# Causal head attention: two of three key blocks centred on GpSimd, two PSUM banks swapped by sequence, four engines reordered

## The chip, the cores and the metric

The program runs on one core of a Trainium2 chip. The metric is the device time of one execution in microseconds (us). The engines are named as in the profile: PE is TensorE (matrix multiplications and transposes; PEld its weight loads), DVE is VectorE, ACT is ScalarE, POOL is GpSimd, SP is SyncE, which issues the DMAs. Each engine works through its own instructions in order, and waits on semaphores for the others.

## The reference, cut to what matters

The whole program is two transformer layers on 16 sequences of 256 tokens with 128 features. The change is inside the first attention only (`_L0_attn_ref`), which has 16 heads of 8 features and a causal mask; its output is added to `x`.

```python
def _L0_attn_ref(x, Wq, Wk, Wv, Wo):       # B=16, T=256, D_MODEL=128, N_HEADS=16, D_HEAD=8
    ...
            scores = scale * jnp.einsum('bhtd,bhsd->bhts', Q, kb)
            scores = jnp.where(future[None, None], -jnp.inf, scores)
            m_new = jnp.maximum(m, jnp.max(scores, axis=-1, keepdims=True))
            p = jnp.exp(scores - m_new)
            ...
            l = corr * l + jnp.sum(p, axis=-1, keepdims=True)
            acc = corr * acc + jnp.einsum('bhts,bhsd->bhtd', p, vb)
    ...
    return acc / jnp.maximum(l, 1e-12)     # then the projection with Wo
...
x = L0_attn_x
x = x + _L0_attn_ref(_layernorm(x, axis=-1), L0_attn_Wq, L0_attn_Wk, L0_attn_Wv, L0_attn_Wo)
```

## The kernel before

The function `head_attention` works through 16 sequences (b) of 4 rounds (j) each, so 64 rounds; a round does 4 of the 16 heads, which lie in 4 groups of 32 partitions. Queries are cut in two tiles of 128. Tile 0 sees key block 0 only, tile 1 sees blocks 0 and 1, so a round has three blocks of 128 keys for each of its 4 heads: 128 partitions x 4 x 384 values. In the tile `a_sc` they are numbered 0 (tile 0, diagonal), 1 (tile 1, key block 0, which needs no mask) and 2 (tile 1, diagonal).

The stages of one round r, with the lines of the profile:

- PE L371 computes the scores into PSUM banks 0 to 3 (16 products).
- DVE L456 adds the mask to blocks 0 and 2 and writes them to `a_sc`; ACT L511 copies block 1 there.
- DVE L444 takes the maxima of block 0 and L446 those of blocks 1 and 2. POOL L330 subtracts the maxima from block 0; DVE L448 subtracts them from blocks 1 and 2 (1024 values in each partition).
- ACT L507 takes the exponential of all three blocks.
- PE L357 transposes the result in three parts of 4 blocks; ACT L496 copies each part out of PSUM. Parts 0 and 2 share bank 4, part 1 has bank 5.
- PE L399 multiplies by the values and by ones (for the sums), and accumulates four rounds in bank 7, which L390 first clears.

Once in a sequence come the projections, all in bank 6: PE L339 and L340 (queries and keys), taken out by ACT L472 and L474 (five instructions); PE L347 (values), taken out by ACT L480; and at the end of a sequence ACT L487 and L489 (the inverse of the sums as logarithm and exponential), DVE L438 (`oT`, the product of accumulator and inverse), PE L414 (the output projection) and DVE L463 (the addition to `xT`). POOL L316 copies a sequence's input.

There is no scheduler. Each engine has its function `iteration`, whose written order is the order of its instructions, and `pipeline` calls it for every round. Rounds overlap by their lag: in the iteration of round r, PE does the scores of r, transposes r-2 and multiplies r-3 by the values; DVE does the maxima and the subtraction of r-1 and then the mask of r; ACT takes parts 0 and 1 of r-2, then the exponential of r-1, the copy of block 1 of r, and part 2 of r-2. In the text the iteration with j=3 is called the sequence's last, although the values of its fourth round are accumulated only in the iteration j=2 of the next one. There are two buffers each of `a_sc`, `a_pr` and `a_prT`, so the mask of r waits for the exponential of r-2 (`exped`).

Waits that matter here: the scores of r wait for the block 1 copy of r-1 (`copied`); the transposes of parts 0 and 1 wait for the exponential of their round and for part 2 of the round before (`taken`); the second maximum waits for the copy; the exponential waits for both subtractions (`centred0`, `centred1`); `oT` waits for the inverse.

Of the kernel before, what the change touches and what calls it, by code (L numbers as in the profile page):

```python
# [265 lines left out]
def head_attention(nc, sem, sb, xT, norm, banks, ident, w, head_mask, mask):  # L266
# [20 lines left out]
    def pipeline(eng, iteration):  # L287

        def one(j, k, b, live, more):
            iteration(j, k, b, lambda lag: b * ROUNDS + (j - lag + 1), live, more)  # L290
        for b in range(2):
            for j in range(ROUNDS):
                one(j, b, b, lambda lag: lag <= b * ROUNDS + j, True)
        with eng.Fori(1, B // 2 - 1) as i:
            for k in range(2):
                for j in range(ROUNDS):
                    one(j, k, i * 2 + k, lambda lag: True, True)
        for b in range(B - 2, B):
            for j in range(ROUNDS):
                one(j, b % 2, b, lambda lag: True, b < B - 1)  # L300
        for j in range(ROUNDS):
            one(j, 0, B, lambda lag: lag > j, False)
# [4 lines left out]
    with nc.Block() as block:  # L307
        @block.gpsimd
        def _(pool):
# [8 lines left out]
            nc.gpsimd.tensor_copy(xa[0][:], norm[:, 0:T]).then_inc(S["xcopy"], 1)  # L318

            def iteration(j, k, b, n, live, more):  # L320
                if more and j == 0:
                    if live(3):
                        copy(b + 1, 1 - k)
                    else:
                        nc.gpsimd.tensor_copy(xa[1 - k][:], norm[:, (b + 1) * T:(b + 2) * T])\
                            .then_inc(S["xcopy"], 1)
                if live(1):
# [4 lines left out]
                        .then_inc(S["centred0"], 1)  # L332
            pipeline(pool, iteration)

        @block.tensor
        def _(pe):
            def project(b, k):
                pe.wait_ge(S["xcopy"], passed(b + 1))
                nc.tensor.matmul(banks[:, 6, 0:T], w[:, 0, :], xa[k][:], start=True, stop=True)  # L339
                nc.tensor.matmul(banks[:, 6, T:2 * T], w[:, 1, :], xa[k][:], start=True, stop=True)\  # L340
                    .then_inc(S["proj"], 1)

            def project_values(b, k):
                pe.wait_ge(S["qmasked"], passed(b + 1))
                pe.sem_inc(sem("gate"), 1)
                for t in range(TILES):
                    last = nc.tensor.matmul(banks[:, 6, t * P:(t + 1) * P], xa[k][:, t * P:(t + 1) * P], w[:, 2, :],  # L347
# [3 lines left out]
            def iteration(j, k, b, n, live, more):  # L351
# [9 lines left out]

                if live(0):
# [20 lines left out]
                if live(3):  # L383
                    pe.wait_ge(S["taken"], passed(n(3) * 3))
                    if j3 == 0:
                        pe.wait_ge(S["vtaken"], passed((b if j == 3 else b - 1) + 1))
                        if live(7):
                            pe.wait_ge(S["odone"], passed(b if j == 3 else b - 1))
                        pe.sem_inc(sem("gate"), 1)
                        nc.tensor.matmul(banks[:, 7, :], zeros[:, 0:64].bitcast(BF16), zeros[:].bitcast(BF16),  # L390
                                         start=True, stop=False)
                    pe.sem_inc(sem("gate"), 1)
                    for t in range(TILES):
                        for add_up in range(2):
                            for s in range(4):
# [4 lines left out]
                                    banks[32 * s:32 * s + 32, 7, lo:lo + (2 - t) * P], stationary,  # L400
# [3 lines left out]
                if more and j == 1:  # L404
                    if live(5):
                        pe.wait_ge(S["added"], passed(b - 1))
                    project(b + 1, 1 - k)
                if more and j == 2:
                    project_values(b + 1, 1 - k)
                if live(4) and j == 3:  # L410
                    pe.wait_ge(S["odone"], passed(b))
                    pe.wait_ge(S["vtaken"], passed(b + 2 if more else B))
                    pe.sem_inc(sem("gate"), 1)
                    nc.tensor.matmul(banks[:, 6, 0:T], w[:, 3, :], oT[:], start=True, stop=True)\  # L414
# [12 lines left out]
        def _(dve):  # L427
# [4 lines left out]

            def iteration(j, k, b, n, live, more):
                if live(4) and j == 3:
                    dve.wait_ge(S["inverse"], passed(b))
                    if live(8):
                        dve.wait_ge(S["wo_done"], passed(b - 1))
                    nc.vector.tensor_tensor(oT[:], banks[:, 7, 0:T], rtotal[:], ALU.mult).then_inc(S["odone"], 1)  # L438
                if live(1):
                    c = (j - 1) % 2  # L440
                    dve.wait_ge(S["masked"], passed(n(1)))
                    if live(3):
                        dve.wait_ge(S["centred0"], passed(n(3)))
# [4 lines left out]
                    nc.vector.tensor_tensor(sc[c][:, :, P:3 * P], sc[c][:, :, P:3 * P],  # L448
                                            mx[c][:, 1].unsqueeze(2).broadcast_to([P, 4, 2 * P]), ALU.subtract)\
# [10 lines left out]
                if live(4) and j == 3:  # L460
                    dve.wait_ge(S["wo_done"], passed(b))
                    rows = xT[:, bass.ds(b - 1, 1), PAD:PAD + T].rearrange("p b t -> p (b t)")
                    nc.vector.tensor_tensor(rows, rows, banks[:, 6, 0:T], ALU.add).then_inc(S["added"], 1)  # L463
# [3 lines left out]
        def _(act):  # L467
            nc.scalar.preload_act_table_set("natural_log_exp_and_others")

            def take_queries_keys(b, k):  # L470
                act.wait_ge(S["proj"], passed(b + 1))
                nc.scalar.activation(kT[k][:], banks[:, 6, T:2 * T], ACT.Copy)  # L472
                for r in range(ROUNDS):
                    last = nc.scalar.activation(qm[k][:, r, :], banks[:, 6, 0:T], ACT.Copy,  # L474
# [3 lines left out]
            def take_values(b, k):  # L478
# [3 lines left out]
                    banks[:, 6, 0:TILES * P].rearrange("p (s j d) -> p s j d", j=ROUNDS, d=AD), ACT.Copy)\  # L482
                    .then_inc(S["vtaken"], 1)

            def invert(b):
                act.wait_ge(S["valued"], passed(b * ROUNDS))
                nc.scalar.activation(rtotal[:], banks[:, 7, T:2 * T], ACT.Ln).then_inc(S["logged"], 1)  # L487
# [3 lines left out]
            def iteration(j, k, b, n, live, more):  # L491
# [6 lines left out]

                if live(2):
# [4 lines left out]
                if live(1):  # L504
                    act.wait_ge(S["centred0"], passed(n(1)))
                    act.wait_ge(S["centred1"], passed(n(1)))
# [1059 lines left out]
```

## Time and profile before

| what | value |
|---|---|
| time, median of 3 runs | 4096.82 us (4094.83 to 4099.13) |
| the profiled execution, its own time | 4096.23 us |
| its span | 4094.3 us |
| head attention, from its first product to the last addition | 48.75 to 425.30 us, 376.55 us |
| busy in that stretch: PE, DVE, ACT, POOL | 307.19, 283.00, 266.95, 71.52 us |
| granted clock of TensorE in that stretch | 0.93 of full speed |
| granted clock in the rest (425.30 to 4094.30 us) | 0.99 |

The changed stage is 9% of the span. No engine is busy throughout in it. The profiled time is what the device took; the span runs from the first to the last recorded instruction, and 1.9 us lie around it. In the timeline rows, `x8` means that eight instructions of one kind in a row are merged, the second number is the length of that merged piece, and the number in brackets is the idle time of that engine before it, with the instruction that ended it. Start times of neighbouring rows on one engine give the true rate, since the next instruction is started a little before the record of the last one ends.

### The profile page before, as it was taken

Reading aid. Unit: us, or ns where it says so; the run is one execution under the profiler, and the core shown is the slowest. Engines: PE = TensorE matmul, PEld = TensorE weight load, DVE = VectorE, ACT = ScalarE, POOL = GpSimd, SP = SyncE. Lnnn points to the kernel's source line nnn. Section 1 sums busy time; section 2 is a strip of 40 time slices with the busy share of each in tenths; the row PEclk is TensorE's granted clock in tenths of the full one; section 3 lists DMA queues with packets and bytes.
Section 4 is the critical chain, followed back from the end, with each engine's and each line's share of the span. In section 5 each row is a group of like instructions: output and inputs, shape, how many; then the busy total and the mean of one; then the engine's idle time right before and its main releaser. Section 6 shows DMA issues by size and latency. Waiting matters only on the chain. (4 is left out here: it accounts for less than half of the span.)

```text
span 4094.3 us, 155009 instructions
## 1 busy us (share of the span) xinstructions
PE 3825.7 (93%) x61323; PEld 2408.6 (59%) x61339; DVE 3160.2 (77%) x4956; ACT 2971.3 (73%) x6599; POOL 2421.4 (59%) x2354
## 2 busy tenths in 40 slices
PE   5888688899999999999999999999999999999998
PEld 3555477466654666645666546666456665466663
DVE  4777455799975899947999658999489996699984
ACT  4777221788876888867888768888678887688885
POOL 2121133588862788826888538888178885378870
PEclk8999899899999999999999999999999999999999
DMA  2000000000000000000000000000000000000000
GB/s 74 0 0 1 0 0 0 7 0 0 0 22 6 1 0 0 0 21 7 0 0 0 21 6 0 0 0 0 22 7 0 0 0 21 7 0 0 0 19 24
DMA packets 12345, 27.32 MB, mean 7 GB/s; under 512 B 2461, under 2 KB 6729, under 8 KB 11345
## 3 DMA queue, kind: packets, MB, share of 16 engines
q1 hardware_dynamic: 12240, 25.72, 1.8%
q8 instruction: 91, 1.49, 0.2%
q14 instruction: 14, 0.11, 0.0%
HBM read 23.62 MB, written 2.10 MB: 6 GB/s over the span
## 5 line engine op out<-in xcount | busy, mean ns | idle before, releaser
L945 POOL TENSOR_TENSOR w_t<-w_t 128x512 f32<-128x512 f32 x768 | 978.4, 1283 | 514.3 <-DVE w_t L1247 514.3
L1247 DVE TENSOR_TENSOR w_t<-banks,w_tab 128x512 f32<-128x512 f32 x1536 | 955.9, 684 | 234.4 <-ACT w_sq L1385 225.7
L961 POOL TENSOR_TENSOR w_t<-w_t,w_rn 128x512 f32<-128x512 f32 x768 | 784.3, 1042 | 252.3 <-ACT w_rn L1422 252.3
L1039 PE MATMUL banks<-w_qk,w_xs 128*128 128x512 f32 x1536 | 825.6, 620 | 7.6 <-issue 6.5
L1059 PE MATMUL banks<-w_vo,w_xs 128*32 128x256 f32 x12288 | 822.8, 385 | 4.9 <-ACT w_us L1376 4.9
L1047 PEld LDWEIGHTS banks<-ident,w_t 128*128 128x128 f32 x3072 | 380.1, 140 | 432.7 <-issue 413.6
L1376 ACT ACTIVATE w_us<-banks 128x512 f32<-128x512 f32 x768 | 456.7, 595 | 161.7 <-PE banks L1059 157.0
L1047 PE MATMUL banks<-ident,w_t 128*128 128x128 f32 x3072 | 461.7, 273 | 25.6 <-POOL w_t L961 16.7
L1284 DVE TENSOR_REDUCE w_ss<-w_sq 128x16 f32<-128x1024 f32 x384 | 464.9, 1211 | 0.0
L1059 PEld LDWEIGHTS banks<-w_vo,w_xs 128*32 128x32 f32 x12288 | 321.6, 109 | 242.7 <-issue 77.0
L966 POOL TENSOR_TENSOR w_pr<-w_pr,w_rl 128x512 f32<-128x512 f32 x384 | 402.3, 1048 | 85.6 <-ACT w_rl L1427 85.6
L1098 PE MATMUL banks<-w_us,w_prT 128*32 128x128 f32 x10752 | 407.7, 273 | 6.1 <-issue 6.1
L1117 PEld LDWEIGHTS banks<-w_kT,w_qT 64*32 64x32 f32 x24576 | 319.1, 105 | 160.2 <-issue 160.2
L1098 PEld LDWEIGHTS banks<-w_us,w_prT 128*32 128x32 f32 x10752 | 349.1, 110 | 81.0 <-issue 18.9
L1117 PE MATMUL banks<-w_kT,w_qT 64*32 64x64 f32 x24576 | 381.2, 219 | 0.0
L1385 ACT ACTIVATE w_sq<-banks 128x512 f32<-128x512 f32 x384 | 229.2, 597 | 198.9 <-PE banks L1039 189.3
L1265 DVE TENSOR_TENSOR w_pr<-banks,w_mx 128x256 f32<-128x256 f32 x768 | 290.4, 420 | 22.1
L1288 DVE TENSOR_REDUCE w_tot<-w_pr 128x8 f32<-128x512 f32 x384 | 263.4, 686 | 56.6 <-ACT w_pr L1414 37.3
L1019 PE MATMUL banks<-logv,m_w 128*114 128x512 f32 x576 | 280.0, 622 | 23.1 <-DVE logv L1224 23.1
L1393 ACT ACTIVATE w_sq<-banks 128x512 f32<-128x512 f32 x384 | 229.7, 598 | 82.7 <-PE banks L1039 82.7
L1039 PEld LDWEIGHTS banks<-w_qk,w_xs 128*128 128x128 f32 x1536 | 231.1, 190 | 94.1 <-issue 94.1
L1259 DVE TENSOR_REDUCE w_mx<-banks 128x8 f32<-128x512 f32 x384 | 265.6, 692 | 13.0
(178 smaller groups left out, 5940.1 us busy)
## 6 DMA issues: line engine op xcount, KB each, us to landing
w_qk<-w_qk_in SPq DMA_DIRECT2D x7, 1024.0 KB, 4.8
w_v<-w_v_in SPq DMA_DIRECT2D x7, 512.0 KB, 5.6
w_o<-w_o_in SPq DMA_DIRECT2D x7, 512.0 KB, 6.3
m_w<-m_w_in SPq DMA_DIRECT2D x6, 342.0 KB
xT<-x_in SPq DMA_DIRECT2D x4, 512.0 KB
out<-kept SPq DMA_DIRECT2D x8, 256.0 KB, 2.4
m_w<-m_w_in SPq DMA_DIRECT2D x6, 171.0 KB
r_tab<-r_tab_in SPq DMA_DIRECT2D x1, 512.0 KB
```

What stands on the lines that cost most here:

```text
L945: nc.gpsimd.tensor_tensor(v1, v1, v2[:, :, ::-1, :], ALU.add).then_inc(S["added"], 1)
L961: nc.gpsimd.tensor_tensor(v1, v1, rn[j % 2][:, i * HALF:(i + 1) * HALF].unsqueeze(2) .broadcast_to([P, HALF, WD]), ALU.mult).then_inc(S["n ...
L966: nc.gpsimd.tensor_tensor(p[:], p[:], rl[j % 2][:].unsqueeze(1).unsqueeze(3) .broadcast_to([P, 2, HALF, WIN]), ALU.mult).then_inc(S["weigh ...
L1039: nc.tensor.matmul(banks[:, i, :], x[:], wqk[:, i * INNER + hh * C:i * INNER + (hh + 1) * C], start=True, stop=True).then_inc(S["qk"], 1)
L1047: last = nc.tensor.transpose(banks[:, 3 + i, g * P:(g + 1) * P], t1[j1 % 2][:, lo:lo + P], ident[:])
L1059: last = nc.tensor.matmul(banks[WIN * g:WIN * (g + 1), 2, lo:lo + 2 * P], x[:, WIN * w:WIN * (w + 1)], wvo[:, first:first + 2, :].rearrang ...
L1098: last = nc.tensor.matmul(banks[WIN * w:WIN * (w + 1), 7, 0:P], prT[:, chunk, WIN * w:WIN * (w + 1)], rhs, start=(hv == 0 and i == 0), sto ...
L1117: last = nc.tensor.matmul(bank[WIN * w:WIN * (w + 1), g], qT[j1 % 2][rows, g, WIN * w:WIN * (w + 1)], kT[rows, hk * NPAIR + g, lo:lo + 2 * ...
L1247: nc.vector.tensor_tensor(dst[j % 2][:, i * C:(i + 1) * C].rearrange("p (h d) -> p h d", d=WD), src, tab[:, 2 * t + cs, i * WD:(i + 1) * W ...
L1265: nc.vector.tensor_tensor(pr[j2 % 2][:, :, par * NPAIR:(par + 1) * NPAIR].rearrange("p a g r -> p g a r"), heads[:, par], mx[j2 % 2][:, pa ...
L1284: nc.vector.tensor_reduce(ss[j % 2][:], sq[:].rearrange("p a h d -> p (a h) d"), AX, ALU.add)\
L1376: nc.scalar.activation(us[j][:, 2 * a:2 * a + 2].rearrange("p w a n -> p (w a n)"), banks[:, 2, :], ACT.Copy).then_inc(S["u_taken"], 1)
```

## The change

It touches only `head_attention`.

- **Subtraction.** POOL subtracts from block 0 and from block 1 (two instructions of 512 values in each partition, new L327 and L331), DVE only from block 2 (512 values, new L451). `centred0` counts two for each round.
- **Banks.** The accumulator of a sequence with buffer k lies in bank 6+k, and the projections for it lie in bank 7-k. The output projection goes to the bank that the sequence's own accumulator had.
- **POOL.** The inputs of two sequences are copied ahead, not of one.
- **ACT.** The block 1 copy of r comes before the exponential of r-1, not after it. The inverse moves from the end of iteration j=2 to the head of iteration j=3, where it stands before the copies of the transposed parts (the same place in the stream).
- **PE.** The query and key projections of the next sequence move from the tail of iteration j=1 to the head of j=2, before the scores. The part 2 transposes come before the value projection and the output projection, not after them.
- **DVE.** `oT` moves from the head of iteration j=3 to its tail, after the mask. The addition to `xT` moves to the head of iteration j=2 of the sequence after the next.

The core of the diff:

```diff
@@ gpsimd
+            for b in range(2):
+                nc.gpsimd.tensor_copy(xa[b][:], norm[:, b * T:(b + 1) * T]).then_inc(S["xcopy"], 1)
...
+                if more == 2 and j == 0:
+                    copy(b + 2, k)
                 if live(1):
...
+                    pool.wait_ge(S["maxed"], passed(n(1) * 2))
+                    nc.gpsimd.tensor_tensor(sc[c][:, :, P:2 * P], sc[c][:, :, P:2 * P],
+                                            mx[c][:, 1].unsqueeze(2).broadcast_to([P, 4, P]), ALU.subtract)\
+                        .then_inc(S["centred0"], 1)
@@ tensor
+                if more and j == 2:
+                    if live(6):
+                        pe.wait_ge(S["added"], passed(b - 1))
+                    project(b + 1, 1 - k)
                 if live(0):
...
-                        nc.tensor.matmul(banks[:, 7, :], zeros[:, 0:64].bitcast(BF16), zeros[:].bitcast(BF16),
+                        nc.tensor.matmul(banks[:, 6 + k3, :], zeros[:, 0:64].bitcast(BF16), zeros[:].bitcast(BF16),
...
-                if more and j == 1:
-                    if live(5):
-                        pe.wait_ge(S["added"], passed(b - 1))
-                    project(b + 1, 1 - k)
+                if live(2):
+                    pe.wait_ge(S["taken"], passed(n(2) * 3 - 2))
+                    pe.sem_inc(sem("gate"), 1)
+                    turn(2)
                 if more and j == 2:
                     project_values(b + 1, 1 - k)
                 if live(4) and j == 3:
                     pe.wait_ge(S["odone"], passed(b))
-                    pe.wait_ge(S["vtaken"], passed(b + 2 if more else B))
...
-                if live(2):
-                    pe.wait_ge(S["taken"], passed(n(2) * 3 - 2))
-                    pe.sem_inc(sem("gate"), 1)
-                    turn(2)
@@ vector
+            def add(b, k):
+                dve.wait_ge(S["wo_done"], passed(b + 1))
+                rows = xT[:, bass.ds(b, 1), PAD:PAD + T].rearrange("p b t -> p (b t)")
+                nc.vector.tensor_tensor(rows, rows, banks[:, 6 + k, 0:T], ALU.add).then_inc(S["added"], 1)
...
+                if j == 2 and live(10):
+                    add(b - 2, k)
...
-                    nc.vector.tensor_tensor(sc[c][:, :, P:3 * P], sc[c][:, :, P:3 * P],
-                                            mx[c][:, 1].unsqueeze(2).broadcast_to([P, 4, 2 * P]), ALU.subtract)\
+                    nc.vector.tensor_tensor(sc[c][:, :, 2 * P:3 * P], sc[c][:, :, 2 * P:3 * P],
+                                            mx[c][:, 1].unsqueeze(2).broadcast_to([P, 4, P]), ALU.subtract)\
...
+                if j == 3 and not live(0):
+                    add(b - 1, 1 - k)
```

ACT, inside the loop, from the part 2 copy of iteration j=2 to that of iteration j=3 (`a_v`: values, `a_rtotal`: logarithm and inverse, `a_prT`: transposed parts, `a_pr`: exponential, `a_sc`: block 1). Before:

```order
L496 ACTIVATE a_prT<-banks 128x512 [waits a_turned]
L480 ACTIVATE a_v<-banks 128x32x8 [waits a_vproj]
L487 ACTIVATE a_rtotal<-banks 128x256 [waits a_valued,a_odone]
L489 ACTIVATE a_rtotal<-a_rtotal 128x256 [waits a_logged]
L496 ACTIVATE a_prT<-banks 128x512 [waits a_turned] x2
L507 ACTIVATE a_pr<-a_sc 128x1536 [waits a_centred1,a_centred0]
L511 ACTIVATE a_sc<-banks 128x4x128 [waits a_masked]
```

Changed:

```order
L502 ACTIVATE a_prT<-banks 128x512 [waits a_turned]
L486 ACTIVATE a_v<-banks 128x32x8 [waits a_vproj]
L493 ACTIVATE a_rtotal<-banks 128x256 [waits a_valued,a_odone]
L495 ACTIVATE a_rtotal<-a_rtotal 128x256 [waits a_logged]
L502 ACTIVATE a_prT<-banks 128x512 [waits a_turned] x2
L516 ACTIVATE a_sc<-banks 128x4x128 [waits a_masked]
L521 ACTIVATE a_pr<-a_sc 128x1536 [waits a_centred1,a_centred0]
```

Only the last two have changed places; the inverse stands where it stood.

DVE, inside the loop, iteration j=3 of a sequence (`a_mx`: maxima, `a_oT`: the product with the inverse). Before:

```order
L438 TENSOR_TENSOR a_oT<-banks,a_rtotal 128x256 [waits a_wo_done,a_inverse]
L444 TENSOR_REDUCE a_mx<-a_sc 128x4 [waits a_centred0,a_masked]
L446 TENSOR_REDUCE a_mx<-a_sc 128x4 [waits a_copied]
L448 TENSOR_TENSOR a_sc<-a_sc,a_mx 128x4x256 [waits a_maxed]
L456 TENSOR_TENSOR a_sc<-banks,a_mask 128x4x2x128 [waits a_exped,a_scored]
L463 ISA [waits a_wo_done]
L463 TENSOR_TENSOR xT<-xT,banks 128x256
```

Changed:

```order
L447 TENSOR_REDUCE a_mx<-a_sc 128x4 [waits a_centred0,a_masked]
L449 TENSOR_REDUCE a_mx<-a_sc 128x4 [waits a_copied]
L451 TENSOR_TENSOR a_sc<-a_sc,a_mx 128x4x128 [waits a_maxed]
L459 TENSOR_TENSOR a_sc<-banks,a_mask 128x4x2x128 [waits a_exped,a_scored]
L467 TENSOR_TENSOR a_oT<-banks,a_rtotal 128x256 [waits a_wo_done,a_inverse]
```

`oT`, which stood ahead of the maxima, stands behind the mask, the subtraction is half as wide, and the addition has left this iteration.

## Rows read from the trace of the kernel before

**Rows 1.** The profile's page, its first line.

```profile
span 4094.3 us, 155009 instructions
```

**Rows 2.** Windows: length; busy (instructions) of PE, PEld, DVE, ACT, POOL; PE's clock; DMA.

```profile
48.75:425.30 376.55, 307.19 (x4000) 214.96 (x4016) 283.00 (x288) 266.95 (x448) 71.52 (x79) 0.93 0.00 1
84.97:401.71 316.74, 261.97 (x3495) 183.81 (x3498) 246.72 (x252) 231.32 (x388) 62.65 (x69) 0.95 0.00 1
203.20:226.11 22.91, 19.38 (x252) 13.39 (x252) 17.68 (x19) 16.75 (x28) 4.50 (x5) 0.93 0.00 0
226.11:248.13 22.02, 17.82 (x252) 12.64 (x252) 17.69 (x19) 16.53 (x28) 4.50 (x5) 1.00 0.00 0
```

**Rows 3.** Timeline of ACT, 224 to 244 us: start, length, engine, line, instruction, [idle before].

```profile
224.23 0.66 ACT L496 ACTIVATE a_prT<-banks 128x512 f32<-128x512 f32 x1
...
226.11 1.09 ACT L496 ACTIVATE a_prT<-banks 128x512 f32<-128x512 f32 x2 [0.22 <-PE banks L357]
...
233.24 1.09 ACT L496 ACTIVATE a_prT<-banks 128x512 f32<-128x512 f32 x2 [1.22 <-PE banks L357]
234.21 1.49 ACT L507 ACTIVATE a_pr<-a_sc 128x1536 f32<-128x1536 f32 x1
235.59 0.60 ACT L511 ACTIVATE a_sc<-banks 128x512 f32<-128x512 f32 x1
236.06 0.61 ACT L496 ACTIVATE a_prT<-banks 128x512 f32<-128x512 f32 x1
237.89 1.09 ACT L496 ACTIVATE a_prT<-banks 128x512 f32<-128x512 f32 x2 [1.22 <-PE banks L357]
...
241.26 0.60 ACT L496 ACTIVATE a_prT<-banks 128x512 f32<-128x512 f32 x1 [0.43 <-PE banks L357]
...
243.45 1.12 ACT L496 ACTIVATE a_prT<-banks 128x512 f32<-128x512 f32 x2
```

**Rows 4.** The same timeline, DVE and POOL, 225 to 240 us.

```profile
225.92 0.42 DVE L438 TENSOR_TENSOR a_oT<-banks,a_rtotal 128x256 f32<-128x256 f32 x1 [3.46 <-ACT a_rtotal L489]
...
228.00 0.40 POOL L316 COPY a_x<-norm 128x256 f32 x1
228.10 1.38 DVE L448 TENSOR_TENSOR a_sc<-a_sc,a_mx 128x1024 f32<-128x1024 f32 x1
...
235.98 1.04 POOL L330 TENSOR_TENSOR a_sc<-a_sc,a_mx 128x512 f32<-128x512 f32 x1 [3.33 <-DVE a_mx L444]
...
236.22 1.22 DVE L446 TENSOR_REDUCE a_mx<-a_sc 128x4 f32<-128x1024 f32 x1 [0.31 <-ACT a_sc L511]
...
237.47 1.23 DVE L448 TENSOR_TENSOR a_sc<-a_sc,a_mx 128x1024 f32<-128x1024 f32 x1
...
238.61 1.22 DVE L456 TENSOR_TENSOR a_sc<-banks,a_mask 128x1024 f32<-128x1024 f32 x1
...
239.86 0.69 DVE L444 TENSOR_REDUCE a_mx<-a_sc 128x4 f32<-128x512 f32 x1
```

**Rows 5.** The same timeline, PE, 228 to 243 us.

```profile
228.38 0.70 PE L414 MATMUL banks<-a_oT,a_w 128*128 128x256 f32 x2
...
232.55 1.09 PE L357 MATMUL banks<-ident,a_pr 128*128 128x128 f32 x8
...
235.01 0.66 PE L357 MATMUL banks<-ident,a_pr 128*128 128x128 f32 x4
...
239.66 0.70 PE L339 MATMUL banks<-a_x,a_w 128*128 128x256 f32 x2
...
240.63 0.60 PE L357 MATMUL banks<-ident,a_pr 128*128 128x128 f32 x4
241.16 0.94 PE L371 MATMUL banks<-a_kT,a_qm 32*128 32x128 f32 x16
242.03 1.09 PE L357 MATMUL banks<-ident,a_pr 128*128 128x128 f32 x8
```

**Rows 6.** The page's groups of instructions: forms, count | busy us, mean ns | idle before.

```profile
L1247 DVE TENSOR_TENSOR w_t<-banks,w_tab 128x512 f32<-128x512 f32 x1536 | 955.9, 684 | 234.4 <-ACT w_sq L1385 225.7
```

More of the change, by code:

```diff
@@ L292, in pipeline @@
             for j in range(ROUNDS):
-                one(j, b, b, lambda lag: lag <= b * ROUNDS + j, True)
+                one(j, b, b, lambda lag: lag <= b * ROUNDS + j, 2)
         with eng.Fori(1, B // 2 - 1) as i:
@@ L337, in project @@
             def project(b, k):
+                bank = 7 - k
                 pe.wait_ge(S["xcopy"], passed(b + 1))
-                nc.tensor.matmul(banks[:, 6, 0:T], w[:, 0, :], xa[k][:], start=True, stop=True)
-                nc.tensor.matmul(banks[:, 6, T:2 * T], w[:, 1, :], xa[k][:], start=True, stop=True)\
+                nc.tensor.matmul(banks[:, bank, 0:T], w[:, 0, :], xa[k][:], start=True, stop=True)
+                nc.tensor.matmul(banks[:, bank, T:2 * T], w[:, 1, :], xa[k][:], start=True, stop=True)\
                     .then_inc(S["proj"], 1)
@@ L460, in iteration @@
                 if live(4) and j == 3:
-                    dve.wait_ge(S["wo_done"], passed(b))
-                    rows = xT[:, bass.ds(b - 1, 1), PAD:PAD + T].rearrange("p b t -> p (b t)")
-                    nc.vector.tensor_tensor(rows, rows, banks[:, 6, 0:T], ALU.add).then_inc(S["added"], 1)
+                    dve.wait_ge(S["inverse"], passed(b))
+                    if live(8):
+                        dve.wait_ge(S["wo_done"], passed(b - 1))
+                    nc.vector.tensor_tensor(oT[:], banks[:, 7 - k, 0:T], rtotal[:], ALU.mult).then_inc(S["odone"], 1)
+                if j == 3 and not live(0):
+                    add(b - 1, 1 - k)
             pipeline(dve, iteration)
@@ L471, in take_queries_keys @@
                 act.wait_ge(S["proj"], passed(b + 1))
-                nc.scalar.activation(kT[k][:], banks[:, 6, T:2 * T], ACT.Copy)
+                nc.scalar.activation(kT[k][:], banks[:, 7 - k, T:2 * T], ACT.Copy)
                 for r in range(ROUNDS):
-                    last = nc.scalar.activation(qm[k][:, r, :], banks[:, 6, 0:T], ACT.Copy,
+                    last = nc.scalar.activation(qm[k][:, r, :], banks[:, 7 - k, 0:T], ACT.Copy,
                                                 scale=head_mask[:, r:r + 1])
@@ L497, in take @@
                                          banks[:, 4 + part % 2, :], ACT.Copy).then_inc(S["taken"], 1)
+                if live(4) and j == 3:
+                    if live(8):
+                        act.wait_ge(S["odone"], passed(b - 1))
+                    invert(b, 1 - k)
                 if live(2):
@@ L512, in iteration @@
                         .then_inc(S["copied"], 1)
+                if live(1):
+                    act.wait_ge(S["centred0"], passed(n(1) * 2))
+                    act.wait_ge(S["centred1"], passed(n(1)))
+                    nc.scalar.activation(columns(pr[j1 % 2]), columns(sc[j1 % 2]), ACT.Exp, scale=A_SCALE)\
+                        .then_inc(S["exped"], 1)
                 if live(2):
```

47 lines of the change are left out of this document (13 added, 34 removed).

## The prediction, made before the changed kernel ran

> **What bounds the kernel now.** I read the page's first line for the whole [rows 1], then windows to find the stage, then its timeline for one sequence. The stage that is changed takes 376.55 of 4094.3 us, and everything behind it starts when it ends, so a microsecond saved here is one saved in all. In the stage no engine is full: PE is busy 307 of 376.55 us, DVE 283, ACT 267 [rows 2]. So waits set the pace, and the question is which. The second window runs from one copy of part 0 (iteration j=2 of the second sequence) to the same copy 14 sequences later: 316.74/14 = 22.62 us for a sequence. The third and fourth show single sequences: 22.91 us where PE's granted clock was 0.93, 22.02 us where it was 1.00 [rows 2]. A sequence without a clock dip is therefore 22.02 us, with 17.82 us of PE work, 17.69 of DVE and 16.53 of ACT.
>
> Cut at the ACT copies of parts 0 and 1, this sequence has rounds of 7.13 us (226.11 to 233.24), 4.65 (to 237.89), 5.56 (to 243.45) and the rest, 4.68 (to 248.13, the end of the fourth window) [rows 2, 3].
>
> The plain round, 4.65 us, is a ring of DVE and ACT: second maximum 1.25 (236.22 to 237.47), subtraction 1.14 (to 238.61), exponential, block 1 copy, second maximum. ACT stands idle 1.22 us in it [rows 3, 4]. The exponential starts 0.97 us after the part copies although its data are ready about then, and the block 1 copy, on which both the next maximum and the next scores wait, is queued behind it.
>
> The long round, 7.13 us, comes from the inverse. `oT` stands at the head of DVE's iteration, and DVE is idle for 3.46 us before it [rows 4], because ACT reaches logarithm and inverse only behind the exponential, the copy, part 2 and the values. After that stall the whole softmax of the round is late, and PE with it.
>
> **The change, part by part.** *The ring on ACT and PE.* With the copy ahead of the exponential, the DVE part leaves the ring, and the ring that is left is this one: part 2 copy, PE transposes parts 0 and 1, ACT copies them, block 1 copy, exponential, part 2 copy. Its pieces: the part 2 copy lasts 0.60 (241.26 to 241.86), PE starts 0.17 later (242.03), ACT can start 0.69 after PE (232.55 to 233.24) [rows 3, 5]; the two copies 0.97 (233.24 to 234.21), the block 1 copy 0.47 (235.59 to 236.06), the exponential 1.38 (234.21 to 235.59) [rows 3]. The sum is 4.28 us for a plain round against 4.65.
>
> *The other three rounds by the same ring.* In iteration j=1 the query and key copies fill the gap between part 2 and part 0: 2.19 us from one to the other (241.26 to 243.45) in place of 1.46, so 4.28 + 0.73 = 5.01 [rows 3]. The projections now stand behind part 2's transposes on PE, which makes them ready about 0.15 later than ACT wants them (an estimate from PE's pieces below): I take 5.16. In j=2 the values and the inverse fill the gap: 1.88 us (224.23 to 226.11), of which 0.22 is a wait for PE [rows 3] that the earlier scores take away, so 1.66: 4.28 + 0.20 = 4.48. In j=3 ACT alone would give 4.28. PE is late there: its plain round is 2.46 (232.55 to 235.01) + 0.53 (240.63 to 241.16) + 0.87 (241.16 to 242.03) = 3.86; the output projection with 0.70 and its overlap [rows 5], taken at 0.53, and the clearing of the bank, at about 0.3 from the same kind of gaps, make 4.7 against a start that is up to 0.15 early from the round before. I take 4.55. Sum: 4.28 + 5.16 + 4.48 + 4.55 = 18.47, say **18.5 us for a sequence**. PE's 17.82 us is the floor under it [rows 2].
>
> *`oT` and the addition.* At the tail of j=3 the inverse is long there, since ACT makes it before part 0 of that iteration and DVE reaches `oT` after a maximum, another, a subtraction and a mask. The stall of 3.46 us is gone and not replaced: what is queued behind the new wait is the next maximum (0.63 us of work that has 0.5 us to spare). What is late next is the output projection, which now waits for `oT` behind the mask, and the scores of the next round behind it on PE. By the positions above the mask ends 0.3 us after part 0's copy starts, `oT` 0.42 us later, PE wants it at 2.5: covered by well over 1 us. If that cover were gone, each 0.1 us would cost 0.1 us once in a sequence. The deferred addition (0.42 us) releases the projections at the head of j=2; it ends about 0.9 us after part 0's copy, PE arrives at 2.3. Cost nothing, cover 1.2 us.
>
> *DVE's load.* A round is now 0.63 + 1.25 + x + 1.25, the last from mask to maximum (238.61 to 239.86) [rows 4], with x the subtraction of 512 values. The trace has none with this form. Half of 1.14 is 0.57; the 128x512 form from PSUM took 0.684 [rows 6]. I take 0.65, the nearer in shape, and the ends are 0.57 and 1.14 (no gain at all). DVE needs 3.8 us (3.7 to 4.3) of 4.28, so even the upper end is only just a bound. The mask is done 0.57 us before ACT comes to its copy.
>
> *GpSimd.* It gets 1.04 us more in each round [rows 4], 2.1 of 4.28 and the input copy of 0.40. The second subtraction starts with the end of the second maximum, at 2.9 after part 0's copy, and ends at 4.0; the exponential of that round starts at 4.28 + 1.44 = 5.7. The cover is 1.7 us, so its price is nothing, unless it holds up DVE (below). Both subtractions are released by the same maximum: DVE starts 0.03 us after it (237.44 to 237.47), POOL some 0.07 after its own (235.91 to 235.98) [rows 4], so DVE is first. POOL held up by DVE's 0.65 us would still be in time.
>
> In the trace one DVE subtraction met a POOL instruction: the input copy ran from 228.00 to 228.40, and the subtraction that started at 228.10 took 1.38 us in place of 1.23 [rows 4], 0.15 more for 0.30 of overlap. The Trainium skill (SBUF — State Buffer, section "SBUF: two separate sides") says that a VectorE operation with two SBUF inputs and a GpSimd operation that reads SBUF exclude each other for the whole instruction, and that the one that starts first has it. By this rule the row should show the full 0.30; it shows half of it. Under the rule DVE's new subtraction is such an operation and GpSimd's second one starts beside it, so the sum would be the same where DVE is first, and the first rival below where GpSimd is.
>
> *PE's clock.* The third window shows a sequence with a dip (0.93), the fourth one without; the dips cost 22.62 - 22.02 = 0.60 us a sequence in the mean [rows 2]. PE's idle time in a sequence falls from 22.02 - 17.82 = 4.2 us to 0.7, and what starved it longest (the 3.46 us stall of DVE) is gone. I take these 0.60 us as gained. Kept, they would cost 14 x 0.6 = 8 us.
>
> *The sum.* 14 sequences x (22.62 - 18.5) = 57.7 us. Outside that window are 59.8 us [rows 1, 2], the fill and the drain, with about seven rounds in which 0.3 to 0.4 us each is saved, and one more inverse whose stall goes (taken at 2): 5 us, with 2 to 7 as its ends. The start has also a reverse: the first exponential now waits for GpSimd's second subtraction, about 1 us. Together 62 us. The profiled execution took 4096.2 us; 4096.2 - 62 = 4034.2, and its time is 0.6 below the median, so about **4035 us**. Its own range: from 18.1 us for a sequence (ACT's ring without PE's two delays), 4029, to 19.0 us, 4042.
>
> **The rivals.**
>
> *GpSimd first.* If GpSimd's second subtraction holds DVE's up, a ring over DVE appears: block 1 copy 0.60, second maximum 1.25, 0.07 + 1.04 for GpSimd, subtraction 0.65, mask 1.25: 4.86 us a round. A sequence is then 3 x 4.86 + 5.16 + 0.4 for `oT` = 20.1, the gain 14 x 2.5 + 3 = 38, the time 4059. For it: the 0.15 us above. Against it: DVE's earlier start, and that an overlap cost half of itself. Chance 15%. The rule of the Trainium skill named above is this rival's mechanism.
>
> *Waits that add up.* With PE at 17.82 of 18.5 us there is little room, and each handover that is 0.05 to 0.1 us longer than in my rows shifts the ring. At 19.5 us a sequence: 14 x 3.1 + 4 = 47, the time 4049. Branches of the loop (six times in 14 sequences), now hidden in PE's idle stretch, would be in the open as well. Chance 17%.
>
> *The clock stays low: slower.* PE becomes the bound; work at the lower of its two levels, 1.2 GHz in place of 2.4, takes twice as long. 17.82 x (1 + f) = 22.62 gives f = 0.27: if over 27% of the stage's PE work ran at the lower level, the kernel would be slower than before; at 50% a sequence is 26.7 and the time 4096 + 14 x 4.1 = 4153. Against it: a sequence in which PE was busy for only 17.82 of 22.02 us ran at 1.00 [rows 2], and the ones to come leave PE less idle time. Chance 4%.
>
> *The change doesn't remove the stall but moves it.* If the output projection waited for `oT` as long as `oT` waited for the inverse, a sequence would be about 22 us and the time within 8 us of before. My positions leave over 1 us of cover. Chance 4%.
>
> **How the numbers follow.** Forecast 4035 with 60%, GpSimd first (4059) 15%, added waits (4049) 17%, clock 4%, moved stall 4%. The range takes the forecast's lower end, 4028, and reaches over the first two rivals to 4060; what is left out is the slower cases and the extremes of the others, under 2 in 10. A measurement of this kernel can tell about 0.2%, 8 us, from no change. Faster by more than that: all but the last two rivals and a margin, 0.92; within it 0.03; slower 0.05.
>
> **What the profile of the changed kernel would show.** A stage of about 315 us; a sequence of 18.5 us between copies of part 0; no idle time of DVE before `oT`; plain rounds of 4.3 us with ACT idle 0.86 us before part 0 and PE idle 0.4; the second maximum, not the subtraction, as DVE's waiting place; PE's clock above 0.97 after the first sequence; the two GpSimd subtractions at 1.04 us, the second perhaps 0.6 longer. It is wrong if DVE's narrow subtraction shows more than 1 us (the first rival), if PE's clock falls below 0.9, or if the output projection is what ends PE's longest waits.

## The result and the profile after

The changed kernel takes 4026.10 us (median of 4 runs, 4023.78 to 4030.75), the kernel before 4095.82 us (median of 4, 4091.16 to 4099.13). The ratio is 0.983, with a 95% interval of 0.982 to 0.985. That is 69.7 us less, where 62 were forecast, and 1.9 us below the lower end of the stated range (4028).

The profiled execution took 4030.75 us, the slowest of the four. The windows of its trace, cut as in [rows 2]; columns are the window, its length, then busy time and instructions of PE, PEld, DVE, ACT and POOL, and PE's clock:

```profile
48.62:355.00 306.38, 286.75 (x4000) 199.85 (x4016) 250.33 (x288) 260.49 (x448) 170.46 (x143) 0.98 0.00 1
82.06:335.20 253.14, 244.78 (x3497) 171.57 (x3510) 218.89 (x253) 225.46 (x389) 148.70 (x124) 1.00 0.00 1
203.86:221.97 18.11, 17.55 (x252) 12.30 (x252) 15.64 (x19) 16.21 (x28) 10.67 (x10) 1.00 0.00 0
355.00:4028.80 3673.80, 3506.00 (x57291) 2188.42 (x57291) 2865.16 (x4645) 2692.10 (x6132) 2339.26 (x2260) 0.98 0.02 5
```

The stage fell from 376.55 to 306.38 us, by 70.2, which is the whole difference of the medians. The 14 sequences of the second window take 253.14/14 = 18.08 us each in place of 22.62, which gives 63.5 us; fill and drain, outside it, went from 59.8 to 53.2 us and give the other 6.6. PE is busy 97% of that window at a clock of 1.00, where it was 0.95. The rest of the program took 3673.8 us in this execution and 3669.0 in the profiled one of before; the other three executions have spans 4.6 to 7.0 us shorter, so nothing is explained by that.

One sequence on ACT (start, length, instruction, idle time before it), the counterpart of [rows 3]:

```profile
202.44 0.61 ACT L502 ACTIVATE a_prT<-banks 128x512 f32<-128x512 f32 x1
203.86 1.09 ACT L502 ACTIVATE a_prT<-banks 128x512 f32<-128x512 f32 x2 [0.81 <-PE banks L359]
204.83 0.60 ACT L516 ACTIVATE a_sc<-banks 128x512 f32<-128x512 f32 x1
205.31 1.50 ACT L521 ACTIVATE a_pr<-a_sc 128x1536 f32<-128x1536 f32 x1
206.68 0.61 ACT L502 ACTIVATE a_prT<-banks 128x512 f32<-128x512 f32 x1
...
208.89 1.11 ACT L502 ACTIVATE a_prT<-banks 128x512 f32<-128x512 f32 x2
...
211.70 0.66 ACT L502 ACTIVATE a_prT<-banks 128x512 f32<-128x512 f32 x1
...
213.26 1.07 ACT L502 ACTIVATE a_prT<-banks 128x512 f32<-128x512 f32 x2
...
217.73 1.09 ACT L502 ACTIVATE a_prT<-banks 128x512 f32<-128x512 f32 x2 [1.06 <-PE banks L359]
```

The rounds are 5.03 us (203.86 to 208.89), 4.37 (to 213.26), 4.47 (to 217.73) and 4.24 (to 221.97, the end of the third window). They had been 5.56, 4.68, 7.13 and 4.65. The block 1 copy follows the part copies at once, and ACT's only idle time is in front of part 0.

DVE and POOL in the same stretch, the counterpart of [rows 4]:

```profile
202.48 0.69 DVE L451 TENSOR_TENSOR a_sc<-a_sc,a_mx 128x512 f32<-128x512 f32 x1
202.52 1.55 POOL L331 TENSOR_TENSOR a_sc<-a_sc,a_mx 128x512 f32<-128x512 f32 x1 [0.28 <-DVE a_mx L449]
...
212.44 1.23 DVE L459 TENSOR_TENSOR a_sc<-banks,a_mask 128x1024 f32<-128x1024 f32 x1
...
213.58 0.41 DVE L467 TENSOR_TENSOR a_oT<-banks,a_rtotal 128x256 f32<-128x256 f32 x1
```

`oT` starts without any idle time before it; its 3.46 us are gone. GpSimd's second subtraction takes 1.55 us where the first takes 1.04: it starts 0.04 us after DVE's and is stretched by it, while DVE's takes 0.69.

### The profile page after: what moved, and what is told of

It reads as the page before. It is cut to its first block and busy times, and to the rows that moved or that the text cites. A ratio compares the mean times of both kernels' runs of the same rounds, so it can differ in the third digit from the quotient of the medians.

```text
span 4028.8 us, 155156 instructions
## 1 busy us (share of the span) xinstructions
PE 3808.7 (95%) x61323; PEld 2394.8 (59%) x61339; DVE 3127.4 (78%) x4956; ACT 2966.2 (74%) x6599; POOL 2520.9 (63%) x2418
```

## Experiments

Each was run beside the kernel before on the same chip. The changed kernel's 18.1 us for a sequence and 4026.1 us in all are what single undone parts are to be held against. "For a sequence" is the mean distance, in the trace, between the part 0 copies of iteration j=2 over 14 sequences, the first of them the short first sequence; for the changed kernel this mean is 18.10, for the kernel before 22.48. The rest of the program, which no run changes, took 3663 to 3674 us in the fourteen profiled executions, and the median of the kernel before was 4095.0 to 4099.2 us beside the different experiments. So a difference of a few us between two medians tells little, and the length of the stage in the trace (first product to last addition, 306.4 us in the changed kernel) tells more.

**DVE subtracts two blocks again.**

```diff
-  gpsimd: second subtraction, block 1
-  vector: sc[c][:, :, 2 * P:3 * P] -= mx[c][:, 1]
+  vector: sc[c][:, :, P:3 * P] -= mx[c][:, 1]
```

> The changed kernel with one part undone: DVE subtracts blocks 1 and 2 again (1024 values in each partition), GpSimd block 0 only. My theory: the changed kernel runs on a ring of ACT and PE at 18.1 us for a sequence, and DVE has about 0.5 us a round to spare (its own work is 3.8 us a round of 4.2); the wider subtraction takes 0.5 us more, which about fills that. 18.1 to 18.6 us for a sequence, the whole 0 to 8 us slower than the changed kernel (about 4030). Rival, the gain came from the work taken off DVE: then 19.5 us and more for a sequence, over 20 us slower.

4026.94 us, 18.26 us for a sequence. The part that gives the change its name is worth 0.16 us a sequence, 2 us in all, too little for the medians to show; the stage is 309.1 us, 2.8 longer. The rival (DVE's load) is out.

**The exponential first on ACT.**

```diff
-  scalar: copy of block 1 (round r); exponential (round r-1)
+  scalar: exponential (round r-1); copy of block 1 (round r)
```

> The changed kernel with one part undone: ACT takes the exponential before the block 1 copy, as before the change. My theory: the second maximum, GpSimd's subtraction, the exponential and the copy are a ring again, 1.25 + 0.07 + 1.55 + 1.38 + 0.63 = 4.9 us a round in place of 4.24 to 4.47, so about 19.9 us for a sequence and 25 to 30 us more in all (about 4054). Rival, the order on ACT does not matter since the copy is small: within 5 us of the changed kernel.

4051.17 us, 19.78 us for a sequence: 25 us more, as the theory had it. The rounds that begin in j=3 and j=0 are 4.88 and 4.95 us in its trace (208.81 to 213.69 and to 218.64), where 4.9 was expected.

**Fixed banks.**

```diff
-  accumulator in banks[:, 6 + k], projections in banks[:, 7 - k]
+  accumulator in banks[:, 7], projections in banks[:, 6]
-  pe.wait_ge(S["added"], passed(b - 1))      # before clearing the accumulator
+  pe.wait_ge(S["odone"], passed(b if j == 3 else b - 1))
```

> The changed kernel with one part undone: the accumulator is always in bank 7 and all projections in bank 6, so that clearing the accumulator for a new sequence waits for oT of the last one, which now stands behind the mask on DVE. My theory: PE clears the bank at about 214.1 us in the changed kernel's timeline in place of 213.4, and has no slack to make it up: 0.7 to 0.8 us more for a sequence, 18.8 to 18.9, 11 to 13 us in all (about 4038). Rival, the bank swap is idle, since PE would wait there anyway: within 3 us of the changed kernel.

4040.87 us, 18.85 us for a sequence, 0.75 more. The stage is 318.1 us, 11.7 longer, as expected; the median is 14.8 us higher, outside the 11 to 13 expected, with single times from 4035.0 to 4045.2. PE waits for `oT` before it clears the bank (total, times, longest, from 82.92 to 328.88 us):

```profile
PE banks L396 <- DVE a_oT L467: 8.3, 13, 0.7
```

That is 0.64 us a sequence, most of the 0.75. The swap matters, and mostly by the time for which clearing the bank is late.

**`oT` first on DVE.**

```diff
-  vector, j == 3: maxima, subtraction, mask, oT
+  vector, j == 3: oT, maxima, subtraction, mask
```

> The changed kernel with one part undone: oT stands at the head of DVE's iteration j=3 again, ahead of the maxima. My theory: DVE stops for the inverse, which ACT makes just before the part 0 copy of that iteration; the mask of that round is done 3.5 to 3.9 us later than ACT wants it, and that is the larger part of the whole gain: 21.6 to 22 us for a sequence, 52 to 60 us more in all (about 4082). Rival, most of the gain is the shorter ring of every round: then at most 25 us more.

4087.9 us, 22.19 us for a sequence: 61.8 us more, nearly all of the gain back. Its longest waits (who waited, for whom; total, times, longest), from 90 to 380 us:

```profile
DVE a_oT L446 <- ACT a_rtotal L495: 53.1, 13, 4.1
...
ACT a_sc L516 <- DVE a_sc L464: 40.3, 13, 3.1
...
PE banks L377 <- ACT a_sc L516: 23.1, 12, 1.9
```

The stall passes from DVE to the block 1 copy on ACT and on to PE's scores: 4.1, 3.1, 1.9 us. The sequence is a little longer than expected, and PE's clock fell again in some sequences. The windows of two of them, one without a fall and one with:

```profile
173.76:194.83 21.07, 17.82 (x253) 12.35 (x251) 15.40 (x19) 16.32 (x29) 10.70 (x9) 1.00 0.00 0
217.15:240.53 23.38, 20.47 (x253) 13.85 (x251) 15.50 (x19) 16.54 (x29) 10.69 (x9) 0.85 0.00 0
```

At 1.00 the sequence is 21.07 us, and with the dip it is 23.38.

**GpSimd subtracts all three blocks.**

```diff
-  gpsimd: sc[c][:, :, P:2 * P] -= mx[c][:, 1];  vector: sc[c][:, :, 2 * P:3 * P] -= mx[c][:, 1]
+  gpsimd: sc[c][:, :, P:3 * P] -= mx[c][:, 1]
```

> The changed kernel with GpSimd subtracting blocks 1 and 2 as well as block 0 and DVE none. It removes the overlap of a DVE subtraction with a GpSimd one. My theory: the exponential has 2.9 us from the end of the second maximum, GpSimd needs 0.07 + about 2.1 us, and DVE's time is not on the ring: 18.0 to 18.1 us for a sequence, within 3 us of the changed kernel. Rival, GpSimd holds up DVE or the exponential in the changed kernel: then this differs by more than 5 us, faster where DVE was held up, slower where GpSimd's time is on the path.

4024.44 us, 18.10 us for a sequence, the same as the changed kernel. The groups of this run (mean ns after the bar), then of the changed kernel, from 60 to 340 us:

```profile
L331 POOL TENSOR_TENSOR a_sc<-a_sc,a_mx 128x1024 f32<-128x1024 f32 x63 | 119.2, 1893 | 30.6 <-DVE a_mx L449 30.3
```

```profile
L331 POOL TENSOR_TENSOR a_sc<-a_sc,a_mx 128x512 f32<-128x512 f32 x63 | 97.3, 1545 | 29.7 <-DVE a_mx L449 29.5
L327 POOL TENSOR_TENSOR a_sc<-a_sc,a_mx 128x512 f32<-128x512 f32 x62 | 64.5, 1040 | 85.0 <-DVE a_mx L447 85.0
...
L451 DVE TENSOR_TENSOR a_sc<-a_sc,a_mx 128x512 f32<-128x512 f32 x62 | 42.9, 692 | 2.1
```

Without a DVE subtraction beside it, GpSimd does twice the width in 1.89 us; beside one it needs 1.55 for the single width. Neither shows in the time.

**One more ACT instruction, on the ring and in the gap.** Both add a copy of constants (512 in each partition) to a spare tile in two of four rounds.

```diff
                     take(0)
                     take(1)
+                    if live(4) and j in (3, 0): copy of constants     # the run "on the ring"
...
                     take(2)
+                if live(4) and j in (3, 0): copy of constants         # the run "in the gap"
```

> The changed kernel with one more ACT instruction (a copy of 512 constants in each partition to a spare tile, about 0.5 us from start to start) in iterations j=3 and j=0, between the part copies and the block 1 copy, which by my theory is on the ring. Theory: each adds its 0.5 us, 1.0 us for a sequence, 14 to 16 us in all (about 4041). Rival, PE alone is the bound, and ACT has slack everywhere: under 5 us in all. Its twin puts the same instruction where ACT is idle.

> The changed kernel with the same extra ACT instruction as its twin on the ring (512 constants, about 0.5 us, in iterations j=3 and j=0), but after the part 2 copy, where ACT stands idle for 0.8 to 1.06 us while PE transposes. Theory: hidden, 18.1 us for a sequence. Rival, ACT's total work is the bound: 19.1 us for a sequence.

On the ring: 4035.85 us, 18.90 us for a sequence. In the gap: 4023.48 us (2 runs), 18.13 us for a sequence. The instruction moves the block 1 copy by 0.52 us each time:

```profile
206.31 1.08 ACT L503 ACTIVATE a_prT<-banks 128x512 f32<-128x512 f32 x2 [0.81 <-PE banks L360]
207.28 0.63 ACT L516 ACTIVATE a_spare<-a_w 128x512 f32<-128x512 f32 x1
207.80 0.60 ACT L519 ACTIVATE a_sc<-banks 128x512 f32<-128x512 f32 x1
```

So the place decides, not ACT's total work. But two of them cost 0.80 us, not 1.04. The round that begins in iteration j=0 grew from 4.24 to 4.76 us, by the full 0.52; the one that begins in j=3 only from 4.47 to 4.74. In that one PE is late anyway behind the output projection, and 0.25 us were hidden. The cost is 9.8 us by the medians, 12.9 by the length of the stage (319.3 us), where 14 to 16 were expected.

**Banks 4 and 5 exchanged from round to round.** Then part 0 goes to the bank that part 1 had in the round before, which is free earlier.

```diff
-  banks[:, 4 + part % 2, ...]
+  banks[:, 4 + (part + j2) % 2, ...]           # transposes and part copies
-                        pe.wait_ge(S["taken"], passed(n(3) * 3))
+                        pe.wait_ge(S["taken"], passed(n(3) * 3 - 1))
                     turn(0)
+                    if live(3): pe.wait_ge(S["taken"], passed(n(3) * 3))
                     turn(1)
```

> The changed kernel with banks 4 and 5 exchanged from round to round, so that the transposes of part 0 need not wait for the part 2 copy of the round before. Theory: this opens the ring (part 2 copy, 0.6, and its handover no longer stand before PE's transposes), and PE's own work of 17.8 us is the bound: 17.8 to 17.9 us for a sequence in place of 18.08, 3 to 5 us faster in all (about 4022). Rival, the ring is not closed through the part 2 copy: no change in the sequence's time.

4014.67 us (4013.28 to 4015.81), ratio to before 0.980 (0.979 to 0.982): the fastest kernel of the study, 11.4 us below the changed one. 17.59 us for a sequence. A long stretch of it and one sequence:

```profile
90.00:310.00 220.00, 219.99 (x3140) 153.70 (x3136) 194.59 (x226) 201.74 (x349) 133.42 (x112) 1.00 0.00 0
205.55:223.17 17.62, 17.62 (x253) 12.30 (x251) 15.55 (x19) 16.22 (x29) 10.70 (x9) 1.00 0.00 0
```

PE has no idle time at all there. So the ring did close through the part 2 copy, and behind it PE is the bound, at 17.6 us and not at the 17.82 that I had taken as its floor. The stage is 297.2 us, 9.2 shorter: 14 x 0.52 = 7.3 lie in the sequences, where 3 to 5 were expected, and 1.9 in fill and drain. The other 2.2 us of the difference of the medians do not lie in the stage that was changed, and nothing here explains them.

**The kernel before with `oT` alone moved.**

```diff
   kernel before, vector:
-  j == 3: oT, maxima, subtraction, mask, addition to xT
+  j == 3: maxima, subtraction, mask, oT;   next j == 0: ..., mask, addition to xT
```

> The kernel before with one part of the change alone: oT at the tail of DVE's iteration j=3, and the addition to xT one iteration later; banks, subtraction and all other orders as before. Theory: DVE's stall of 3.46 us goes, the plain ring of 4.65 us stays, and PE waits some 0.5 us for oT before it clears the bank: 19.6 to 20.1 us for a sequence in place of 22.6, 38 to 45 us faster than before (about 4055). Rival, the stall only moves to PE because of the shared bank: within 10 us of before.

4099.02 us, 22.65 us for a sequence: nothing gained (the kernel before took 4095.0 beside it), where I had expected 38 to 45 us. The rival held, and the timeline shows how:

```profile
203.50 1.22 DVE L456 TENSOR_TENSOR a_sc<-banks,a_mask 128x1024 f32<-128x1024 f32 x1
...
204.63 0.41 DVE L464 TENSOR_TENSOR a_oT<-banks,a_rtotal 128x256 f32<-128x256 f32 x1
...
205.19 0.38 PE L390 MATMUL banks<-a_zeros 128*128 128x512 bf16 x1 [2.02 <-DVE a_oT L464]
...
205.49 1.07 PE L399 MATMUL banks<-a_prT,a_v 128*32 128x256 f32 x8
...
209.10 0.60 PE L357 MATMUL banks<-ident,a_pr 128*128 128x128 f32 x4
...
209.74 0.60 ACT L501 ACTIVATE a_prT<-banks 128x512 f32<-128x512 f32 x1 [4.02 <-PE banks L357]
...
210.63 1.22 DVE L456 TENSOR_TENSOR a_sc<-banks,a_mask 128x1024 f32<-128x1024 f32 x1 [2.41 <-PE banks L371]
...
211.52 0.64 PE L399 MATMUL banks<-a_prT,a_v 128*32 128x256 f32 x8
```

PE may not clear the one accumulator bank before `oT` has read it. It stands for 2.02 us, in this sequence its clock then falls (eight products take 1.07 us at 205.49, and 0.64 one round later at 211.52), and the part 2 transposes and the next scores are queued behind all that. The window of this round and that of the next show the clock:

```profile
202.77:211.19 8.42, 6.41 (x65) 4.04 (x64) 5.86 (x7) 3.54 (x5) 1.04 (x1) 0.80 0.00 0
211.19:215.84 4.65, 3.99 (x62) 2.74 (x61) 3.23 (x5) 3.43 (x5) 1.04 (x1) 1.00 0.00 0
```

The wait and the clock have to be kept apart. PE stands 2.0 to 2.2 us for `oT` in each of the thirteen full sequences, but only nine of them have a dip (window clock 0.93, 23.25 to 23.5 us); the other four ran at 1.00 in 21.7 to 21.8 us. One of those, with its wait and its products:

```profile
275.28 0.38 PE L390 MATMUL banks<-a_zeros 128*128 128x512 bf16 x1 [2.13 <-DVE a_oT L464]
275.59 0.64 PE L399 MATMUL banks<-a_prT,a_v 128*32 128x256 f32 x8
```

```profile
268.07:289.85 21.78, 18.05 (x258) 12.61 (x251) 17.61 (x19) 16.52 (x29) 4.50 (x5) 1.00 0.00 0
```

Without a dip the move of `oT` thus gained about 0.3 us (22.02 before). What decides whether the clock dips is not shown.

**The same with the banks swapped.** Nothing else of the change is in it: PE's, ACT's and GpSimd's orders are those of before.

```diff
   on top of the run above:
-  accumulator in banks[:, 7], projections in banks[:, 6]
+  accumulator in banks[:, 6 + k], projections in banks[:, 7 - k]
```

> The kernel before with oT and the addition moved on DVE, as in the run that gained nothing, and now the banks swapped by sequence as well; PE's, ACT's and GpSimd's orders and the subtraction as before. Theory: that run gained nothing because PE stood 2.0 us before clearing the one accumulator bank, its clock then fell, and the part 2 transposes were queued behind all of it; with the swap PE does not stand there, and what is left against the run without the two shorter-ring parts is the part 2 transposes behind the projections: 20.0 to 20.6 us for a sequence, 33 to 42 us faster than before (about 4058). Rival, PE's order is what matters and not the bank: over 22 us for a sequence, within 10 us of before.

4054.59 us, 19.92 us for a sequence: 44.6 us faster than before, 41 by the length of the stage. The two parts together make up about six tenths of the result (2.56 of 4.38 us a sequence). The first gained nothing without the second; the second, the swap without the move of `oT`, was not run. PE's clock is 1.00 from the second sequence on. Against the 21.7 us of a sequence without a dip in the run above the swap gives 1.8 us; the other 0.9 of the 2.73 are the dips that are gone with it.

**The orders and banks without the shorter ring.** The changed kernel with both the first and the second experiment's edits, so PE's order is the new one too.

```diff
-  gpsimd: second subtraction;  scalar: copy, exponential
+  vector: both blocks;         scalar: exponential, copy
```

> The changed kernel with two parts undone: DVE subtracts blocks 1 and 2, and ACT takes the exponential before the block 1 copy. What is left of the change is the place of oT and of the addition, the swapped banks and PE's order. Theory: the stall goes, the old ring over DVE and ACT stays at 4.65 us for a plain round; 19.6 to 20.0 us for a sequence, about 45 us faster than before (about 4052). Rival, which the last single-part run has raised (oT moved alone gained nothing): the orders gain only together with the shorter ring, then over 21 us for a sequence.

4047.05 us, 19.29 us for a sequence. Against the run above, the new order on PE (part 2 before the projections, the query projection one iteration later), with the addition and the input copies at their new places, gives 0.63 us. I had put this run at 19.6 to 20.0.

**Exchange and GpSimd together.**

```diff
   on top of the run with exchanged banks:
-  gpsimd: block 1;  vector: block 2
+  gpsimd: blocks 1 and 2
```

> The changed kernel with banks 4 and 5 exchanged from round to round and GpSimd subtracting all three blocks. Theory: with the exchange PE works without a break in nearly all rounds, so DVE's and GpSimd's share does not count: 17.6 us for a sequence, within 3 us of the run with the exchange alone (about 4014). Rival: with the ring open GpSimd's 3.1 us a round comes onto the path, 5 us and more slower than that run.

4017.56 us, 17.59 us for a sequence: the same sequence as with the exchange alone. Nothing is added.

**The steps in a row**, in us for a sequence:

| kernel | us for a sequence | step | stage, us |
|---|---|---|---|
| before | 22.48 | | 376.6 |
| `oT` and addition moved | 22.65 | +0.17 | 378.8 |
| and banks swapped | 19.92 | -2.73 | 335.2 |
| and PE's new order, with the places of addition and input copy | 19.29 | -0.63 | 325.6 |
| and the copy first on ACT | 18.26 | -1.03 | 309.1 |
| and GpSimd's second block (the changed kernel) | 18.10 | -0.16 | 306.4 |
| and banks 4 and 5 exchanged | 17.59 | -0.51 | 297.2 |

The steps depend on their order. The bank swap is worth 2.73 us in this row of steps, but only 0.75 when it is taken out of the changed kernel (the third experiment). GpSimd's second block without the new order on ACT (the second experiment, 19.78, against 19.29) costs 0.49 us, because its stretched subtraction then stands in the ring between maximum and exponential. In that run's trace the exponential waits for it:

```profile
213.31 1.55 POOL L331 TENSOR_TENSOR a_sc<-a_sc,a_mx 128x512 f32<-128x512 f32 x1 [1.05 <-DVE a_mx L449]
214.97 1.48 ACT L517 ACTIVATE a_pr<-a_sc 128x1536 f32<-128x1536 f32 x1 [0.20 <-POOL a_sc L331]
```

## Why the prediction was wrong in its range, and right in its course

- *Two terms of the sum failed: the length of a sequence, 18.47 us forecast (18.5 in the sum) and 18.08 measured, and fill and drain, 5 - 1 = 4 us forecast and 6.6 measured.* The first is 14 x 0.42 = 5.9 us of the 8 us by which the gain was larger, the second 2.6. The range had room for the first alone: with 18.08 and the forecast fill and drain the time is 4096.2 - 63.5 - 4 = 4028.7. The second took it below 4028. By rounds it was 4.28, 5.16, 4.48 and 4.55 against 4.24, 5.03, 4.37 and 4.47. Two of the allowances were too large: 0.15 us for a late query projection (0.02 came of it, since the round's first gap is 2.21 us against 2.19 before), and 0.27 us for a late PE after the output projection (0.19 came of it, by 4.47 against 4.28; 0.23 against the measured plain round of 4.24). The third, 1.66 us for values and inverse, was read from rows in which ACT had waited. The 0.22 us of idle time count from the end of the inverse's record, and an instruction that need not wait starts 0.10 us before that end: 1.88 - 0.22 - 0.10 = 1.56, which is what the rows show now (211.70 to 213.26).
- *Fill and drain* were 5 us in the forecast, with 7 as the end, and gave 6.6: 2.8 at the start, where I had even set 1 us against the gain, and 3.8 at the end. That the start would lose 1 us to GpSimd's second subtraction does not show; which rounds gave more than forecast was not measured. Both terms came out near their good ends at once, and the range had been built as if only one could. It would have had to reach to 14 x (22.62 - 18.1) + 7 = 70 us, with 4026.
- *The floor of 18.1, "ACT's ring without PE's two delays",* is where it came out, though PE's delay is in it. The floor from PE's own work, 17.82 us, was no floor: the exchanged banks run at 17.6. For the same 253 recorded instructions at a clock of 1.00, PE's busy time is 17.82 us in the run with `oT` first on DVE, where PE stood for 3.25 us in a sequence, and 17.62 where it never stood. So busy time read from a window with waits is a rough floor. Where the 0.2 us come from is not shown.
- *The ring on ACT and PE* was right, in its mechanism and nearly in its size, and three runs bear it out: the old order on ACT costs 1.68 us a sequence, an instruction on the ring costs 0.80 and in the gap nothing, and opening the ring at the part 2 copy frees PE fully.
- *The stall before `oT`* was right as the largest piece (putting it back costs 62 us, dips of the clock included), but the forecast gave it to the place of `oT` alone and priced the bank swap nowhere. It named the wait that takes its place, the output projection's, and missed the other one, the clearing of the accumulator, which the swap does away with. In the changed kernel this made no difference to the sum, since both parts are in it. In the run with one of them it made all the difference.
- *DVE's subtraction* of 512 values takes 0.692 us, forecast 0.65 as the rate from start to start; the next mask starts 0.61 to 0.66 after it where it waits for nothing. DVE's load did not count, as forecast. The sign given for it was half right: DVE waits at the second maximum (40 times, 13.3 us between 82 and 317 us), but as much at the mask for PE's scores (27 times, 14.3 us).
- *GpSimd first* did not happen: DVE was first each time by 0.04 us, GpSimd's subtraction took 0.5 us longer (I had said up to 0.6), and it had the cover that was forecast. The Trainium skill (SBUF — State Buffer, section "SBUF: two separate sides") has the later one blocked until the earlier one is done, here for 0.69 - 0.04 = 0.65 us; the rows show 1.545 - 1.040 = 0.505 us. The direction agrees, the size falls short here as it did with the input copy in [rows 4].
- *PE's clock* was right: 1.00 in the window of 14 sequences. The 8 us for it were counted within the sequence.
- *Waits that add up* did not come: each of the four rounds was shorter than forecast.
- *The slower cases* did not come near. In the experiments on the changed kernel the clock fell only where `oT` was put first again, with waits of PE of up to 1.9 us.

## What to carry to other kernels

When a wait is removed, look for every other user of the resource that its data stood in. The move of `oT` gained nothing on the kernel before until the accumulator had a second bank, so a trial of this part alone would have thrown it out. What a part is worth depends on what stands beside it: the second bank was worth 2.73 us a sequence in one place of the row and 0.75 in another. In a loop over several engines, find the ring that sets the pace by adding or subtracting the handovers as the rows show them. Then ask of each instruction only whether it is in the ring: 0.5 us of ACT work was free in one place and cost 0.3 to 0.5 us in another, and work taken off an engine outside the ring (DVE's block) brought next to nothing. When several allowances of a sum are set on the careful side, they can all come out low together, and the range should let them.

## What the runs showed of the hardware that was not expected

- A GpSimd subtraction of 512 values takes 1.04 us with no DVE subtraction beside it (DVE's second maximum runs then), 1.545 us when DVE's of 0.69 us starts 0.04 us before it, and 1.89 us for 1024 values without a DVE subtraction. DVE's took 0.692 us beside GpSimd's; no run has it without, but a TENSOR_TENSOR of the same width with one input in PSUM takes 0.684 [rows 6].
- In the run with `oT` moved alone PE stood 2.0 to 2.2 us in each full sequence. In the one shown the same eight products then took 1.07 us in place of 0.64, at a window clock of 0.80; but four of thirteen sequences with the same wait ran at 1.00 throughout. A dip made such a sequence about 1.6 us longer (23.3 against 21.7). In the changed kernel, where PE stands at most 0.3 us at a time in the sequence shown, the clock was 1.00 over 253 us; in the run with the banks swapped on top of `oT`'s move it was 1.00 too, with waits of PE of up to 0.9 us.
